# Pair layers: first-unit keys copied by token halves, and the second unit's loads moved from SyncE's queue in the attention to ScalarE's queue in the projections

## The reference, cut to what matters

```python
h = jnp.concatenate([x, latents], axis=1)          # x is the context, latents the stream: 512 keys
q = (latents @ q_w + q_b).reshape(b, k_len, NH, DH)
kv = (h @ kv_w + kv_b).reshape(b, p + k_len, NH, DH, 2)
attn = jnp.einsum('bkhd,bnhd->bhkn', q, kmat) / DH  # DH = 16, NH = 16
attn = softmax(where(full_mask, attn, -inf))
attn_out = jnp.einsum('bhkn,bnhd->bkhd', attn, v) @ out_w + out_b + residual
```

## Time and profile before

| | |
|---|---|
| median of 3 runs | 1305.72 us |
| profiled execution, its own time | 1308.49 us |
| its span, first to last instruction | 1306.7 us |
| mean granted TensorE clock | 0.958 |
| busy: TensorE, VectorE, ScalarE, GpSimd | 93%, 74%, 56%, 39% |
| layer 1 projections, attention | about 714 to 750, 750 to 860 us |
| layer 3 projections, attention | about 1070 to 1124, 1124 to 1235 us |

### The profile page before, as it was taken

One profiled execution on the slowest core, in us unless ns is written; L12 is line 12 of the kernel. 1 busy time (PEld: TensorE's weight loads), 2 busy tenths in 40 slices (PEclk: granted clock), 3 DMA queues, 4 the chain that ended last, 5 costly groups with the idle time before them and its releaser, 6 DMA issues. The chain is left out here.

```text
span 1306.7 us, 27356 instructions
## 1 busy us (share of the span) xinstructions
PE 1211.3 (93%) x9144; PEld 1000.9 (77%) x9144; DVE 968.6 (74%) x2179; ACT 736.1 (56%) x1670; POOL 507.3 (39%) x670
## 2 busy tenths in 40 slices
PE   5999999999799999999889879999899999499989
PEld 4999999999699999999769735558677778255578
DVE  5878787887788788778785468947488876589474
ACT  5665655766466656567662237764166664077651
POOL 4645455444474454554041000122299970001040
PEclk9999999999899999999989959999999999589899
DMA  5210011010211101110030697220384003876021
GB/s 176 58 34 15 27 32 32 24 32 1 101 34 34 33 9 32 32 32 8 1 101 2 129 106 87 41 83 25 89 197 85 2 10 72 127 81 83 2 69 33
DMA packets 56534, 70.90 MB, mean 54 GB/s; under 512 B 6864, under 2 KB 47572, under 8 KB 54104
## 3 DMA queue, kind: packets, MB, share of 16 engines
q1 hardware_dynamic: 54832, 65.83, 24.7%
q10 hardware_dynamic: 1600, 3.76, 1.0%
HBM read 46.79 MB, written 8.13 MB: 42 GB/s over the span
## 5 line engine op out<-in xcount | busy, mean ns | idle before, releaser
L932 ACT ACTIVATE a_prob<-a_s_ps,a_negmax 128x257 f32<-128x257 f32 x256 | 119.0, 476 | 92.8 <-DVE a_negmax L1014 92.8
L2156 DVE TENSOR_REDUCE s_mx<-s_s_ps 128x2 f32<-128x1024 f32 x128 | 152.0, 1211 | 18.3 <-PE s_s_ps L2201 17.9
L2141 ACT ACTIVATE s_probT<-s_st_ps 128x512 f32<-128x512 f32 x256 | 132.2, 606 | 57.7 <-PE s_st_ps L2215 55.4
L873 POOL TENSOR_TENSOR x_v_hi<-a_v_sum,x_one 128x512 fp32r<-128x512 f32 x60 | 63.2, 1054 | 243.8 <-DVE a_v_sum L1003 243.8
L1938 POOL TENSOR_SCALAR s_below<-s_masked,s_mx 128x256 f32<-128x256 f32 x256 | 117.8, 480 | 4.0 <-DVE s_mx L1966 3.1
L1029 DVE TENSOR_TENSOR a_pT_lo<-a_t_ps,a_pT_hi 128x512 fp32r<-128x512 f32 x128 | 88.2, 689 | 37.2 <-ACT a_pT_hi L945 35.5
L1014 DVE TENSOR_REDUCE a_negmax<-a_s_ps 128x2 f32<-128x514 f32 x128 | 86.8, 688 | 23.0 <-PE a_s_ps L1075 22.9
L945 ACT ACTIVATE a_pT_hi<-a_t_ps 128x512 fp32r<-128x512 f32 x128 | 76.7, 599 | 46.7 <-PE a_t_ps L1129 43.1
L2278 POOL TENSOR_TENSOR a_k_high<-x_tok,parts_b_out 128x256 f32<-128x256 f32 x16 | 11.1, 731 | 229.3 <-DMA parts_b_out<-L_xattn_out_b 229.3
L1966 DVE CUSTOM_DVE_ANT_0 s_masked<-s_s_ps,l_mask 128x256 f32<-128x256 f32 x256 | 90.7, 420 | 4.5 <-PE s_s_ps L2003 4.5
L2201 PE MATMUL s_s_ps<-l_k_st,l_q_st 49*128 49x512 f32 x192 | 68.1, 546 | 22.2 <-PEq L2506 10.2
(11 more groups left out here) (348 smaller groups left out, 4039.3 us busy)
## 6 DMA issues: line engine op xcount, KB each, us to landing
a_wo_raw<-L_xattn_wo SPq DMA_DIRECT2D x16, 256.0 KB, 3.3
x_wqk_raw<-L_xattn_wq SPq DMA_DIRECT2D x31, 128.0 KB, 2.3
x_wqk_raw<-L_xattn_wk SPq DMA_DIRECT2D x31, 128.0 KB, 2.3
x_wv_raw<-L_xattn_wv SPq DMA_DIRECT2D x15, 256.0 KB, 3.1
l_k_st<-k_second SPq DMA_DIRECT2D x12, 256.0 KB, 9.8
l_k_st<-k_stack SPq DMA_DIRECT2D x16, 192.0 KB
l_q_st<-q_stack SPq DMA_DIRECT2D x12, 192.0 KB
x_vbias<-L_xattn_bias_v SPq DMA_DIRECT2D x2, 1024.0 KB, 6.5
```

Source lines behind the costliest of these rows:

```text
L932: nc.scalar.activation(prob[:, n % 2, qt, 0:NK], s_ps[:, n % 2, qt, 0:NK], ACT.Exp, bias=negmax[:, n % 2, qt:qt + 1], accum_out=den[:, n % ...
L2141: nc.scalar.activation(probT[:, third % 2, n // 4, n // 2 % 2, n % 2], st_ps[:, u % 3], ACT.Exp, scale=c.scale).then_inc(z.exp_done, 1)
L2156: nc.vector.tensor_reduce(mx[:, i % 2, qt, a::2], s_ps[:, n % 2], AX.X, ALU.max).then_inc(z.max_done, 1)
```

## The change

Four edits, the same in both pair layers where not said otherwise.

- **Keys by halves.** A unit-0 key copy is split by token half: 12 copies of the context half (64 KB, runs of 1 KB) once the context's early keys are ready (`context_k` = 2 groups), 12 of the stream half at `first_k` = 4 groups. 24 key copies in place of 12; query copies as before. In layer 1 groups 0 and 1 are put ahead of the turns on all three engines, as layer 3 has them already.
- **Constant rows awaited last.** SyncE waits for the six constant-row DMAs at the end of the stage, no longer ahead of the copies.
- **Stores by parts.** Context keys are stored before `high` of group 4, stream keys before group 6, queries before group 8: two DMAs each, six in place of four.
- **Loads moved.** The 12 loads of unit 1 are issued by ScalarE's queue at the end of its projection list, after a wait for the six stores to land; they count on a semaphore of their own, `second_loaded`, for which TensorE waits ahead of quad 4. SyncE's list in the attention has nothing in iterations 0 and 1 but the row DMAs.

```diff
+    def load_key_half(self, c, eng, j, src, k_st, sem):
+        a, half = divmod(j, 2)
+        tokens = slice(src * S, (src + 1) * S)
+        for n in range(3):
+            rows = slice(half * c.HALF + n * c.HD, half * c.HALF + (n + 1) * c.HD)
+            eng.dma_start(k_st[rows, a, :, tokens].bitcast(F32),
+                          self.k[(0, 0, 1)[n]][j * c.HD:(j + 1) * c.HD, :, src, :].bitcast(F32)).then_inc(sem, 16)
...
-    def store(self, eng, parts, sem):
+    def store_keys(self, eng, parts, src, sem):
         for part in range(2):
-            eng.dma_start(self.k[part], parts.k[part][P // 2:P].bitcast(F32).rearrange("c b s t -> c (b s t)")
-                          ).then_inc(sem, 16)
+            eng.dma_start(self.k[part].rearrange("c (b s t) -> c b s t", s=2, t=S)[:, :, src, :],
+                          parts.k[part][P // 2:P, :, src, :].bitcast(F32)).then_inc(sem, 16)
+
+    def store_queries(self, eng, parts, sem):
+        for part in range(2):
             eng.dma_start(self.q[part], parts.q[part][P // 2:P].bitcast(F32)).then_inc(sem, 16)
...
-        sp.wait_ge(z.rows_in, 6 * 16)
 
     def copy_first_unit(self, sp):
         c, z = self.c, self.z
-        sp.wait_ge(z.qk_lo, self.first_k)
-        for j in range(4):
-            self.early.load_head(c, sp, 0, j, self.q_st[:, 0], self.k_st[:, 0], z.first_in, "k")
+        for src, count in enumerate((self.context_k, self.first_k)):
+            sp.wait_ge(z.qk_lo, count)
+            for j in range(4):
+                self.early.load_key_half(c, sp, j, src, self.k_st[:, 0], z.first_in)
         sp.wait_ge(z.qk_lo, self.first_q)
         for j in range(4):
             self.early.load_head(c, sp, 0, j, self.q_st[:, 0], self.k_st[:, 0], z.first_in, "q")
-        sp.wait_ge(z.first_in, c.UNIT)
-        sp.wait_ge(z.stored, 4 * 16)
-
-    def store_second_unit(self, act):
-        act.wait_ge(self.z.qk_lo, self.first_q)
-        self.second_unit.store(act, self.early, self.z.stored)
+        sp.wait_ge(z.first_in, 36 * 16)
+        sp.wait_ge(z.stored, 6 * 16)
+        sp.wait_ge(z.rows_in, 6 * 16)
+
+    def store_second_unit(self, act, g):
+        for src, count in enumerate((self.context_k, self.first_k)):
+            if g == count + 2:
+                act.wait_ge(self.z.qk_lo, count)
+                self.second_unit.store_keys(act, self.early, src, self.z.stored)
+        if g == self.first_q + 2:
+            act.wait_ge(self.z.qk_lo, self.first_q)
+            self.second_unit.store_queries(act, self.early, self.z.stored)
+
+    def load_second_unit(self, act):
+        act.wait_ge(self.z.stored, 6 * 16)
+        for is_k, dst in ((True, self.k_st), (False, self.q_st)):
+            self.second_unit.load(self.c, act, is_k, dst[:, 1])
...
             @block.tensor
             def _(pe):
+                for g in range(2):
+                    work.group(pe, g)
                 for n in range(4):
                     work.turn(pe, n)
-                for g in range(len(groups)):
+                for g in range(2, len(groups)):
                     work.group(pe, g)
...
             @block.scalar
             def _(act):
...
-                    if g == work.first_q + 2:
-                        work.store_second_unit(act)
+                    work.store_second_unit(act, g)
                     work.high(act, g)
+                act.wait_ge(z.rows_in, 6 * 16)
+                work.load_second_unit(act)
...
-                    if first in (0, 1):
-                        second_unit.load(c, sp, first == 0, slots[1][first == 0], unit_in[0])
...
-                        pe.wait_ge(unit_in[g - 1], (c.STACKED, c.UNIT + 4 * 16, c.UNIT)[g - 1])
+                        if g == 1:
+                            pe.wait_ge(second_unit.loaded, c.STACKED)
+                        else:
+                            pe.wait_ge(unit_in[g - 1], (c.UNIT + 4 * 16, c.UNIT)[g - 2])
```

More of the change, by code:

```diff
@@ L1528, with __init__, load @@
 class SecondUnit:
-    def __init__(self, core, c):
+    def __init__(self, st, core, c):
+        self.loaded = st.sem("second_loaded")
         self.q = core.nc.dram_tensor(f"q_second{c.layer}", (2, P // 2, T), F32).ap()
         self.k = core.nc.dram_tensor(f"k_second{c.layer}", (2, P // 2, B * c.NK), F32).ap()
-    def store(self, eng, parts, sem):
+    def store_keys(self, eng, parts, src, sem):
         for part in range(2):
-            eng.dma_start(self.k[part], parts.k[part][P // 2:P].bitcast(F32).rearrange("c b s t -> c (b s t)")
-                          ).then_inc(sem, 16)
+            eng.dma_start(self.k[part].rearrange("c (b s t) -> c b s t", s=2, t=S)[:, :, src, :],
+                          parts.k[part][P // 2:P, :, src, :].bitcast(F32)).then_inc(sem, 16)
+    def store_queries(self, eng, parts, sem):
+        for part in range(2):
             eng.dma_start(self.q[part], parts.q[part][P // 2:P].bitcast(F32)).then_inc(sem, 16)
-    def load(self, c, eng, is_k, dst, sem):
+    def load(self, c, eng, is_k, dst):
         stack = (self.k if is_k else self.q).rearrange("u (a s d) n -> u s d a n", s=2, d=c.HD)
@@ L1548, in load @@
                 eng.dma_start(dst[rows].bitcast(F32).rearrange("d a b n -> d a (b n)"), stack[part, half]
-                              ).then_inc(sem, 16)
+                              ).then_inc(self.loaded, 16)
 class PairWork:
@@ L1567, in __init__ @@
         self.tiles = [(src, b) for src in range(2) for b in range(B)]
+        self.context_k = max(n for n, g in enumerate(groups) if g[0] and not g[1] and not g[2]) + 1
         self.first_k = max(n for n, g in enumerate(groups) if g[0] and not g[1]) + 1
@@ L1716, in _ @@
             def _(act):
+                for g in range(2):
+                    work.high(act, g)
                 for n in range(4):
                     work.turned_high(act, n)
-                for g in range(len(groups)):
-                    if g == work.first_q + 2:
-                        work.store_second_unit(act)
+                for g in range(2, len(groups)):
+                    work.store_second_unit(act, g)
                     work.high(act, g)
+                act.wait_ge(z.rows_in, 6 * 16)
+                work.load_second_unit(act)
             @block.vector
             def _(dve):
+                for g in range(2):
+                    work.low(dve, g)
                 for n in range(4):
                     work.turned_low(dve, n)
-                for g in range(len(groups)):
+                for g in range(2, len(groups)):
                     work.low(dve, g)
@@ L2646, in pair_layer @@
             late = HeadParts(st, "late", k_high)
-            second_unit = SecondUnit(core, c)
+            second_unit = SecondUnit(st, core, c)
             if before:
```

## The result

The changed kernel takes 1326.84 us (median of 4 runs, 1321.57 to 1327.9) against 1305.72 (1305.52 to 1306.49) before: ratio 1.0148, 95% interval 1.0128 to 1.0168. Forecast were 1290.6 us with a range of 1279 to 1303. The profiled execution has a span of 1326.1 us (before: 1306.7).

What follows compares the result with a forecast made beforehand. TensorE is nearly always busy but idles 26.5 us at four places, behind SyncE's copies and row DMAs. Earlier starts of 1.4 and 5.1 plus 8.6 from rows give 15.1 us off the median: 1290.6 us, range 1279 to 1303.

Steps and rivals of the forecast that it cites:

- Stores by parts: ScalarE's six store issues in the projections: no stall, 0 us; up to 4 us per layer kept for the range.
- Loads moved: End of both projection stages: loads on ScalarE's queue slow the query copies by 3 us, between 0 and 7.6.
- the step on the rows: Attention's first row DMAs: waits of 5.43 and 5.21 us before the first shifted scores go; 8.6 of 10.6 us counted.
- rival B: Gain halved, by slower copies before the attention (1299.8 us) or rows still waiting inside it (1299.2 us); chance 0.21.
- B's first way: End of both projection stages: query copies take 7.6 us more, starts at 753.0 and 1123.7, gain 5.9 us, total 1299.8.
- its second: Attention's first rows wait as before, loads still in flight on the same engines; gain 6.5 us, total 1299.2.
- C: Both projection stages: ScalarE's load issues at 1.44 to 1.8 us end the stage, +1.7 to +10.3 us; chance 0.09.
- Key halves: Projection stages: each half costs 0.63 us; attention could start at 745.4 in layer 1 and 1116.1 in layer 3.
- Turns: Layer 1's turns behind two groups: TensorE waits about 1.2 us (0 to 2.5) for the split of turned chunks.
- Clock: Attention's first iterations at 0.50: costed at nothing, VectorE bounds them; up to 2 us per layer gained at 1.00.

Runs made afterwards that it cites:

- the three ways of dealing tried here: Second unit's loads spread over more attention iterations on SyncE, with the change's rest or on the kernel before: ratios 1.0011 and 1.0031, 1.006 and 1.0058, 1.0001 and 1.0004.

## Why the prediction was wrong

**The step that failed** is *Loads moved*: "The transfers overlap with the query copies. How much they slow them no row shows ... Above, every copy takes twice its 0.63, 7.6 us for twelve. I take 3 us." Measured were 15.6 and 12.0 us of later starts. Against the forecast of 1.4 and 5.1 us earlier that is 34.1 of the 36.2 us between forecast and result. The kernel with the loads back, which differs by the loads alone, splits them: its projections are 15.9 us shorter in layer 1 and 16.3 in layer 3, where 3 were charged each time, so the loads account for 26.2 of the 34.1 and the key halves (below) for 7.9. The upper bound was built wrongly: it took two flows that share the engines evenly, each copy at half speed, and counted only the twelve query copies. What the runs show is close to one line for both queues: a copy issued behind 2.25 MB lands about when they have gone (to within some 3 us). The loads also came four us sooner than forecast (733.17, not 737, since the last store landed 4.2 us after its issue and not 7.2) and so stood beside key halves too. The bound was the whole 18 us of the loads. All its numbers stood in the prediction, in the step on the rows, which had the loads "still in flight" in layer 3 and the rows waiting for them in rival B; the query copies were not put to the same question. The unused share of 0.72 during the copies, taken as room, belonged to a stretch in which SyncE's issues set the pace and each copy landed 2.4 us after its issue.

What the prediction took from the Trainium skill's page "DMA: Bandwidth & Descriptors", section "Issuing engines are not separate DMA queues" (DMAs of different issuing engines run on the same 16 DMA engines), was right in direction and the result is beyond what I made of it: the landing went from 2.4 to 19.2 us. The same page's section "Back-pressure in remote DMA", on which rival B drew, speaks of transfers between cores, and there are none here.

**The rivals.** B's first way had the right place, the query copies, and charged 7.6 us where 15.9 came; its second, rows that wait, did not happen, since TensorE had waited for the loads before. C, the slower one, was named for another reason and did not happen: ScalarE's issues took 0.54 and 0.64 us, as forecast (0.45 to 0.66), and it was done before the last copy.

**Key halves**: mis-sized. The first went out at 719.55 (forecast 720.5), but 24 of them took until 740.18, 0.86 each and not 0.63, since a half beside the stores costs up to 1.52. The loads-back kernel, which has this edit undisturbed, starts at 749.56 and 1119.68, where 745.4 and 1116.1 were forecast: worth 0.3 us in layer 1 and 4.3 more in layer 3, not 4.4 and 8.1.

**Rows**: the wait went at both places, as forecast, with the idle time before the stage as its price: the loads had landed by then because TensorE had waited for them. The attention became shorter by 2.6 + 5.5 = 8.1 us against 8.6, but that agreement is luck. The 5.43 us of layer 1 gave only 2.6, since TensorE worked twice for 3.4 us at a granted clock of 0.50 near the end of that attention. The same 32 matmuls before and after, and one of the two stretches after:

```profile
853.05 1.92 PE L2228 MATMUL s_ox_ps<-s_probT,l_v_st 128*17 128x256 f32 x32
```

```profile
862.77 3.45 PE L2261 MATMUL s_ox_ps<-s_probT,l_v_st 128*17 128x256 f32 x32
```

```profile
863.00:866.40 3.40, 3.40 (x34) 1.40 (x28) 0.00 (x0) 0.89 (x3) 0.00 (x0) 0.50 0.45 116
```

TensorE was busy throughout, and the kernel before has such stretches at the end of layer 3's attention (1225.8 to 1229.3), so this need not come from the change.

**Turns**: 1.01 us of waiting against 1.2. **Stores by parts**: no stall, as forecast. **Clock**: costed at nothing. The stretch at 0.50 around the start of layer 1's attention grew from 30.7 to 41 us, but within the attention it shrank from 28.9 to 22.5; what it costs was not measured apart.

That the loads, issued early, cause the loss is shown, and that it goes by their bytes. How the engines choose between the two queues is not: single-packet turns (P) fail on the rows, one queue until it is empty (D) fails on the changed kernel's trace, and the order of issue (F) holds only to within some 3 us. Whether the common limit lies in the DMA engines or in the few partitions that all these transfers write was not tried, nor whether a queue fed by GpSimd would stand in the same line. Why a half or a key copy is slower beside the stores is open too.

## What to carry to other kernels

In these runs a second issuing queue (SyncE's beside ScalarE's) gave a DMA no priority and no lane of its own: what decided its landing, to within some 3 us, was how many bytes had been issued ahead of it on either queue. Before a load is moved earlier, list the awaited DMAs that will be issued behind it and charge each of them the load's whole remaining transfer, at the rate of a row of that same load. Where a large load has to go beside small awaited ones, cut it so that its issue paces it, and look which consumer is next in line: in the three ways of dealing tried here part of the wait moved on to the next one.

## What was not expected of the hardware

- A backlog on one queue holds up the other: row DMAs alone on SyncE's queue cost a wait of 10.51 us behind loads of ScalarE's queue, and 0 to 0.17 when those were issued in small pieces. Where both queues had a backlog, both moved (1.67 and 0.41 MB in 17 us).
- The loads from DRAM keep the engines full (share 1.05 to 1.15) at only 131 to 140 GB/s, where copies and stores reached 305. The same key loads in runs of 1 KB moved 99 GB/s at a share of 0.37.
- Copies within the core slow down beside stores to DRAM: up to 1.52 us to issue a 64 KB half against 0.62 alone.
